# Second attention: where TensorE's value products stand among the scores of a step

## The reference

```python
def kernel_func(q, k):
    scores = jnp.einsum('bhqd,bhkd->bhqk', q, k) / jnp.sqrt(jnp.asarray(HD, q.dtype))
    w = jax.nn.relu(scores)
    return w / (jnp.sum(w, axis=-1, keepdims=True) + KERN_EPS)
...
attn = kernel_func(q, k)
out = jnp.einsum('bhqk,bhkd->bhqd', attn, v)
out = out.transpose(0, 2, 1, 3).reshape(Bx, Sx, D)
out = out @ w_out + b_out
y = x + out
mu = jnp.mean(y, axis=-1, keepdims=True)
var = jnp.var(y, axis=-1, keepdims=True)
return (y - mu) * jax.lax.rsqrt(var + LN_EPS) * gamma + beta
```

## Time and profile before

| | us |
|---|---|
| median of 3 runs | 2148.38 |
| lowest and highest | 2147.45, 2151.19 |
| the profiled execution, whole | 2147.88 |
| its span, first to last instruction | 2145.9 |
| PE busy | 2025.3 |
| DVE busy | 1644.6 |
| ACT busy | 1198.5 |
| POOL busy | 925.6 |

### The profile page before, as it was taken

One profiled execution on the slowest core, in us unless ns is written; L12 is line 12 of the kernel. 1 busy time (PEld: TensorE's weight loads), 2 busy tenths in 40 slices (PEclk: granted clock), 3 DMA queues, 4 the chain that ended last, 5 costly groups with the idle time before them and its releaser, 6 DMA issues.

```text
span 2145.9 us, 44877 instructions
## 1 busy us (share of the span) xinstructions
PE 2025.3 (94%) x10800; PEld 1449.4 (68%) x10800; DVE 1644.6 (77%) x3338; ACT 1198.5 (56%) x1737; POOL 925.6 (43%) x904
## 2 busy tenths in 40 slices
PE   2999998999999999999999999998999999999999
PEld 2777777666666577777777777775333347777777
DVE  3777777777777667767758888886677788888887
ACT  3666664555555656666645444444667664454443
POOL 1655555232333356666644444442212234444444
PEclk9999999999999999999999999999999999999999
DMA  4333335223332134344411111112433411111111
GB/s 162 107 104 110 105 103 149 70 80 102 95 98 85 45 112 122 112 117 119 121 40 42 40 49 49 39 45 91 130 106 99 127 36 40 45 44 44 39 49 69
DMA packets 119981, 179.34 MB, mean 84 GB/s; under 512 B 33408, under 2 KB 37856, under 8 KB 119776
## 3 DMA queue, kind: packets, MB, share of 16 engines
q1 hardware_dynamic: 119904, 178.41, 27.5%
HBM read 147.15 MB, written 31.20 MB: 83 GB/s over the span
## 4 chain that ended last, share of the span: by engine, by line
PE 58%; issue 15%; POOL 13%; DVE 9%; ACT 2%; DMA 1%; POOLq 1%; DVEq 1%; SPq 1%; ACTq 0%
PE pair L389 12%; PE pair L391 12%; PE pair L390 11%; POOL h_lo L1305 9%; PE bank L611 4%; PE pair L697 3%; PE pair L719 3%; PE bank L589 2%; PE pair L780 2%; PE bank L389 2%; POOL rstd L1230 1%; DVE rmax L1134 1%; PE bank L391 1%; PE bank L390 1%; PE pair L706 1%
## 5 line engine op out<-in xcount | busy, mean ns | idle before, releaser
L1311 POOL TENSOR_TENSOR h_lo<-hid,h_hi 128x512 fp32r<-128x512 f32 x256 | 333.7, 1304 | 428.4 <-ACT h_hi L873 428.3
L389 PE MATMUL pair<-xnT_hi,w_hi 128*128 (+1 forms) x1056 | 433.2, 410 | 0.8 <-DVE prod L1057 0.8
L1305 POOL TENSOR_TENSOR h_lo<-hid,h_hi 128x512 fp32r<-128x512 f32 x256 | 329.8, 1292 | 228.6 <-ACT h_hi L841 227.3
L391 PE MATMUL pair<-xnT_hi,w_lo 128*128 (+1 forms) x1056 | 418.5, 396 | 0.0
L390 PE MATMUL pair<-xnT_lo,w_hi 128*128 (+1 forms) x1056 | 416.6, 395 | 0.0
L868 ACT ACTIVATE hid<-pair,bias 128x512 f32<-128x512 f32 x256 | 176.5, 689 | 328.1 <-PE pair L391 315.5
L389 PE MATMUL pair<-h_hi,w_hi 128*128 128x512 f32 x784 | 317.9, 405 | 19.1 <-POOL h_lo L1305 9.6
L391 PE MATMUL pair<-h_hi,w_lo 128*128 128x512 f32 x784 | 309.5, 395 | 0.0
L390 PE MATMUL pair<-h_lo,w_hi 128*128 128x512 f32 x784 | 308.2, 393 | 0.0
L1077 DVE TENSOR_SCALAR h_hi<-pair,nb 128x512 fp32r<-128x512 f32 x256 | 191.2, 747 | 83.6 <-PE pair L391 82.7
L1057 DVE SCALAR_TENSOR_TENSOR prod<-pair,bias,wb 128x512 f32<-128x512 f32 x256 | 191.0, 746 | 68.4 <-PE pair L391 55.7
(11 more groups left out here) (164 smaller groups left out, 3246.4 us busy)
## 6 DMA issues: line engine op xcount, KB each, us to landing
wb<-parts_dram SPq DMA_DIRECT2D x512, 128.0 KB, 2.8
wb<-parts_dram SPq DMA_DIRECT2D x128, 256.0 KB, 3.3
parts_dram<-attn_parts SPq DMA_DIRECT2D x96, 256.0 KB, 3.0
attn_q_st<-parts_dram SPq DMA_DIRECT2D x64, 256.0 KB, 2.7
k_one<-parts_dram SPq DMA_DIRECT2D x128, 64.0 KB, 2.4
attn_k_st<-parts_dram SPq DMA_DIRECT2D x32, 256.0 KB, 3.0
stage_w<-in_w_dram SPq DMA_DIRECT2D x32, 130.0 KB, 2.5
stage_w<-in_w_dram SPq DMA_DIRECT2D x6, 512.0 KB, 8.7
```

Source lines behind the costliest of these rows:

```text
L389: eng.matmul(o, w_hi_, v_hi, start=start, stop=False, **kw)
L391: return eng.matmul(o, w_lo_, v_hi, start=False, stop=stop, **kw)
L1305: eng.tensor_tensor(h_lo[:, p % NH0, :], hid[:, unit_of(p) % NHID, :] if p else hs[:, :], h_hi[:, p % NH0, :].bitcast(F32), ALU.subtract). ...
L1311: eng.tensor_tensor(h_lo[:, j % NH1, :], hid[:, j // 2 % NHID, :], h_hi[:, j % NH1, :].bitcast(F32), ALU.subtract).then_inc(lo1p_ready, 1)
```

## The change

The loop over `PV_AT[n]` moves from behind both halves of the scores to between them. It issues the same products with the same waits.

```diff
--- before.py
+++ after.py
@@ -780,11 +780,12 @@
                     ins = eng.matmul(pair[m % NPAIR][:, j, :], mem1.k_st[rows_, quad, kb * P:(kb + 1) * P], mem1.q_st[rows_, quad, :],
                                      start=True, stop=True)
                 ins.then_inc(s1_ps, 1)
-            for m in PV_AT[n]:
-                if m >= 0:
-                    pv1(eng, ch, m)
-                elif not ch.first:
-                    pv1(eng, ch.before(), m + NS1)
+                if h == 0:
+                    for v in PV_AT[n]:
+                        if v >= 0:
+                            pv1(eng, ch, v)
+                        elif not ch.first:
+                            pv1(eng, ch.before(), v + NS1)
 
 
         def act_prep(eng, step, ch):
```

## The result

The changed kernel takes 2162.23 us (median of 4 runs, 2161.8 to 2164.44), the kernel before 2148.01 on the same chips (2147.45 to 2151.19). The ratio is 1.0065 with a 95% interval of 1.0048 to 1.0083: slower by about 14 us, against 2161 forecast. The profiled execution took 2164.44, of which the span is 2162.5. It began the second attention 3.4 us later than the one of before (1488.06 against 1484.61), which the change can't cause; from the first score to the start of the last value product it took 280.15 us against 267.15, so 13.0 more.

The account below looks back on a forecast made before the run. TensorE, busy for 94% of the span, was taken as the bound. A chunk grows by 1.23 + 1.61 - 0.72 = 2.12 us; 2147.9 + 16.8 (8 x 2.1) - 4 for the clock gives 2161 us, range 2151 to 2174.

Parts of the forecast that it names:

- First term: Steps 0 to 3, A(0) to A(4): norm and turn come later, 9.57 us against 8.34, +1.23 a chunk.
- A chain without slack: Steps 0 to 3, behind the norm: GpSimd's root, VectorE's scaling, TensorE's turn, 4.53 us after the norm began.
- Second term: Steps 4 to 9, A(4) to A(10): q, k, v, proj cut pairs; 1.72 - 0.49 + 0.38 = +1.61 us a chunk.
- the wait at A(5): Step 5: TensorE arrives 1.43 us after B(3), VectorE's loop takes 1.81, so a new wait of 0.38.
- The lone half: Steps 4 to 9: a score half cut from its pair costs its own 0.43 us, four times a chunk.
- The rival at 0.22: Steps 4 to 9: lone halves cost 0.22 us each, 6.7 less in all, 2154 us; chance 0.13.
- Third term: Steps 10 to 15, A(10) to next A(0): product fills B(11)'s wait; 9.03 us against 9.75, -0.72 a chunk.
- The clock: Low granted clock, 10.7 us over four slow chunks before; the prediction took 4 us less with the change.
- The first rival: Steps 10 to 13: the gap heals the clock, ScalarE's takes leave no wait; 2139 to 2146 us; chance 0.09.
- the new gap ahead of the turn: Steps 1 to 3: no value product for 3.8 us instead of 2.4, over 1 us of it idle.
- the third rival: Ahead of the turn: the clock falls in every chunk at the new gap, 25 us, 2173 us; chance 0.2.
- The edges: Chunks 0 and 7: each lacks a part but breaks pairs in as many places within one; counted 2.1 us each.

Follow-up runs that it names:

- e9: The change, with GpSimd's last addition of a chunk's result on one of four blocks of tokens only; 2156.67 us, one execution.
- e4: The change, with ScalarE also taking B(15); 2161.60 us, ratio 1.0075 to the kernel before.
- e8: The change, with ScalarE also taking B(15) and GpSimd's last addition on one of four blocks of tokens only; 2150.26 us, one execution.
- e2: The kernel before, with the value product between the halves in steps 4 to 9 only; 2159.71 us, ratio 1.0059.
- e3: The kernel before, with the value product between the halves in step 11 only; 2147.15 us, ratio 1.0002.
- e1: The kernel before, with the value product between the halves in step 15 only; 2163.57 us, ratio 1.0088.
- e10: The change, with ScalarE also taking B(15) and the multiplication by gamma moved from GpSimd to VectorE; 2159.04 us, ratio 1.0057 to the kernel before.
- e13: The kernel before, with ScalarE's double takes in steps 0, 2, 11, 13, 15 and gamma on VectorE; 2147.11 us, ratio 0.9995.
- e6: The kernel before, with ScalarE's double takes in steps 0, 2, 11, 13, 15 in place of 0, 2, 10, 11, 13; 2151.59 us, ratio 1.0023.
- e12: The kernel before, with the multiplication by gamma moved from GpSimd to VectorE; 2146.61 us, ratio 0.9993.
- e5: The kernel before, with the product between the halves in step 11 only and ScalarE's double takes in steps 0, 2, 11, 13, 15; 2152.43 us, ratio 1.0024.
- e11: The kernel before, with step 11's product between the halves, ScalarE's double takes in steps 0, 2, 11, 13, 15 and gamma on VectorE; 2144.21 us, ratio 0.9989.

## Why the prediction was right, and where it wasn't

The time, 2162.23 against 2161, rests on the right order of sizes for a chunk (2.12 forecast, 2.3 measured), on two misses that cancel, and on luck in the first term.

First term (steps 0 to 3): the size came out, 9.57 forecast and 9.6 measured, and the cause is half right. VectorE's late take is one chain, and it alone gives 9.38 (e9); GpSimd's queue ends 0.2 later (e4, e8, e9). "A chain without slack" named the root but not GpSimd's own work ahead of it, which comes later too, and the 1.39 us that GpSimd had waited were read from a chunk that follows one with low clock; behind a chunk at full clock there were 0.21. That the sum is right to 0.03 is luck: the forecast put the norm 1.48 after A(0), it began at 1.28, and the second chain filled the difference.

Second term (steps 4 to 9): right but for 0.14. 15.56 forecast, 15.42 measured, and e2 shows the cut pairs alone at 15.03, without the wait at A(5), which was 0.39 with the change (0.38 forecast).

The lone half: 0.43 forecast, about 0.4 net from e2; from a lone half to the q projection behind it the rows show 0.43 (1605.81 to 1606.24). The rival at 0.22 would have given 14.3 there and is out. That a change of the array's mode drains it, the rule that the prediction took from the Trainium skill ("TensorEngine Tiling (Array Packing)", Key Properties), fits this price; no run here separates a drain from the loss of the side-by-side run.

Third term (steps 10 to 15): 9.03 forecast, 9.24 measured, so -0.5 instead of -0.72. The 0.21 are the wait of A(0). The prediction had it wait for the take of B(14), but the ring starts anew with each chunk, and A(0) waits for that of A(15): ScalarE's three takes from 1624.32 last 2.86 us, to 1627.18, and A(0) starts at 1627.23, 0.40 behind B(15). (The same 0.2 is what the norm began earlier after A(0).) The sentence "This is where the change gives something", with the product filling B(11)'s wait, is wrong for that product alone, which gives nothing (e3), because ScalarE's takes are the bound, which the same paragraph had found. Where the 0.5 comes from can be read from the rows, though no run separates it. In e3 A(12) and B(12) wait one behind the other, 0.38 and 0.41. With the change A(12) waits 0.33, and the product of step 12 runs while ScalarE takes the next half; the row at 1621.95 is then late by 0.40 and the one at 1623.78 not at all, where both of these rows were late before (0.38 and 0.40). The 0.40 of A(0) comes on top.

The clock: the mechanism was right in direction and too small. In the six chunks 1 to 6 the sum was 202.7 us before and is 207.2 now. At 31.97 and 34.27 for a chunk at full clock that leaves 10.9 for low clock before and 1.6 now: 9.3 less, not 4. The first rival had all of it gone, and on this it was nearly right; it failed on its other half, that no wait of ScalarE stays. That the new gap ahead of the turn would bring the low clock back (the third rival) happened in chunk 1, where 3.6 us pass without a product, and in chunk 7, in none of chunks 2 to 6.

The edges: 2.1 each for chunks 0 and 7 was too little. Chunk 0 grew by 2.5 (its clock was 0.89 before and is 0.85) and chunk 7, counted to the start of its last value product, by 6.0 (32.2 at full clock to 38.1 at 0.91), half of it in the first stretch, around the turn. So 13.0 us in the stage is 6 x 2.3 - 9.3 + 8.5, where I had 6 x 2.1 + 4.2 - 4. The gain by the clock was sized 5 us too small and the loss at the edges 4 us too small, and that the two cancel is luck.

## What to carry to other kernels

Instructions that only run side by side while they stand next to each other are one unit: before something is put between them, look for the places where other work already stands on the far side, since each cuts a unit at full price. And a take, copy or turn-out that starts later delays everything in order behind it on its engine; check every queue that ends in the same wait, the one with slack too, and read its slack where the stretch before it ran at full clock (here 0.21, not 1.39). A wait that is filled is gained only if the engine that was waited for isn't itself the bound: here ScalarE's four takes in a row moved the wait on to the next two halves. Where a ring doesn't divide the work of a round, look at the wrap by itself: its waits are other ones.

## What was not expected of the hardware

That the time of one kernel moves so much, and how unevenly two idle places bring the low clock. Between executions of one kernel the time moved by about 12 us (e1: 2155.76 to 2167.79; the kernel before, 30 runs beside e10 to e13, 2138.61 to 2151.25), and in the profiles the clock falls to 0.50 in another set of chunks each time.

But it falls in few places. I counted in which stretches of chunks 1 to 6 the granted clock was under 1.00, in the one profiled execution of each of the 14 kernels. Where B(11) waits 0.88 us behind proj, with its product behind it (the kernel before, e1, e2, e6, e12, e13), that was so in the third stretch of 22 of 36 chunks. Where the product of step 11 stands ahead of B(11) (the change, e3, e4, e5, e8 to e11), it was so in 2 of 48, both in e3. In the first stretch, or just behind it, it was so in 12 of the 42 in which the turn waits 0.6 us or more, in 2 of the 6 of e1, where B(0) waits 1.13, and in none of the other 36. The time without a value product doesn't sort these cases: behind proj it is 3.5 us in the kernel before (four of six), ahead of the turn 3.6 to 3.9 in the change (one of six), with 1.45 of it idle.

That fits what e1 and e2 cost, about as much as the change, 16.5 and 12.6 us by the medians (2147.09 for the kernel before beside them), though a chunk at full clock grows by only 1.3 and 1.1 instead of 2.3: both keep the old wait behind proj and had low clock there in five of six chunks, the change in none. These counts are from one execution each, e1's being its fastest and e2's its slowest. That the change pays for itself in part this way is what the profiles show; why a wait behind proj brings the fall more often than a longer one ahead of the turn is open.
